# The shared expert of two sparse mixtures: four unrolled chunks become one chunk and a loop of three, on three engines, with one buffer of activations

## The chip, the cores and the metric

The kernel runs on one core of one Trainium2 chip (trn2). The metric is the device time of one execution in microseconds. TensorE is called PE here (its weight loads PEld), VectorE DVE, ScalarE ACT, GpSimd POOL and SyncE SP. A trailing q (PEldq, SPq) means the engine's sequencer: waits, register operations, branches and DMA issues.

## What is computed

Four layers of attention and feed-forward on x of 8 x 256 x 256 floats, that is 2048 tokens (16 tiles of 128 tokens) by 256 channels. The change lies in the feed-forward parts of the layers 2 and 3, which are mixtures of experts. Each adds a shared expert, which every token passes, and experts to which tokens are routed:

```python
# layer 2: 2 shared experts of 128 seen as one of 256, 16 routed ones, 2 a token
sh_mid = gelu(einsum('th,ehd->ted', xt, Wsh_up)); shared_out = einsum('ted,edh->th', sh_mid, Wsh_down)
...
routed_out = einsum('ted,edh->th', rt_mid * gate[:, :, None], Wrt_down)
return shared_out + routed_out
# layer 3: shared expert of 352, gated; 32 routed ones of 176, 6 a token
g = ragged_dot(xs, w_gate, group_sizes); u = ragged_dot(xs, w_up, group_sizes)
d = ragged_dot(silu(g) * u, w_down, group_sizes)
...
shared = silu(x @ sw_gate) * (x @ sw_up) @ sw_down
return expert_out + shared
```

## The kernel before

Both mixtures are built by one function, sparse_stage (a configuration for each layer). A stage runs in this order.

1. The normed tokens are transposed into norm_t. PE makes the logits, DVE ranks them and works out, for each token and each of its experts, a slot in a table of rows in DRAM (slot), and which expert each tile of 128 slots belongs to (expert_at).
2. POOL scatters the rows of the tokens into that table with indirect DMAs (L2190), 96 of them in layer 3 (16 tiles by 6 experts), 32 in layer 2. They are counted by the semaphores dispatched.
3. At the same time the shared expert runs on PE, ACT and DVE. The 2048 tokens are cut into 4 chunks of 512. The shared expert's hidden width is cut into SB blocks of 128: SB = 2 in layer 2 (256) and 3 in layer 3 (352). For a chunk c and a block k, shared_up (L1917) multiplies on PE into a PSUM bank: one bank (s_up_bank) in layer 2, two banks (s_gate_bank, then s_up_bank) in layer 3. Banks are double, one or the other by the number of the block. In layer 2 ACT applies Gelu and writes s_hidden (L2000); in layer 3 ACT applies Silu to the gate's bank (L1997) and DVE multiplies with the other bank into s_hidden (L2140). Then shared_down (L1927) multiplies the whole hidden width of the chunk back to 256 channels, in two halves (two banks y_bank, 2 tiles each), and DVE adds each half to x (L2148).
4. When all is there, PE walks through the tiles of routed rows: 47 in layer 2, 127 in layer 3 (transpose_rows L1939, up L1950, transpose_hidden L1958, down L1967). SP loads the rows of the tiles, 12 tiles ahead (L1870). In layer 3 room is short: SP loads the last part of the experts' weights (L1861, 3.4 MB) only after all four chunks of shared_down (wait on s_y_done for 2 * CHUNKS), since the activations of the shared expert lie in its place, and the rows are loaded behind it in SP's queue. In layer 2 SP waits for all blocks of shared_up before it loads rows.

The order of the shared expert's work is written out by shared_steps: up blocks of chunk c, with the down part of chunk c - 1 placed behind the first up block of chunk c. On PE, in layer 3, that is (first number the chunk, second the block): up 0,0; up 0,1; up 0,2; up 1,0; down 0; up 1,1; up 1,2; up 2,0; down 1; up 2,1; up 2,2; up 3,0; down 2; up 3,1; up 3,2; down 3. PE may begin up m (m = c * SB + k) when the block m - 2 has been taken out of its bank (semaphore s_hidden_ready). s_hidden is double, one for even and one for odd chunks. ACT and DVE may write a chunk's hidden block when the down part of the chunk before the last is done (s_y_done).

Signals between engines are semaphores, added to by the last instruction of a piece: s_gate_done and s_up_done by PE for each half of an up block, s_acted_ready by ACT, s_hidden_ready by DVE (by ACT in layer 2), s_y_done by PE for each half of a down part, shared_added by DVE.

A matrix product of two f32 operands is two passes, so the profile shows 2 MATMUL for each nc.tensor.matmul: an up block of layer 3 is x8, of layer 2 x4, a down part x24 and x16.

## Time and profile before

| what | us |
|---|---|
| three runs | 3160.33, 3177.08, 3180.0 |
| median | 3177.08 |
| the profiled execution, whole time | 3163.23 |
| its span in the trace | 3161.1 |

The profile is of one execution; its whole time is 2.1 us longer than the span and lies in the lower part of the range of the three runs. Times in rows are microseconds from the span's start. Layer 2's shared expert runs from about 1615 to 1671, layer 3's from about 2634 to 2796.

### The profile page before, as it was taken

To read this page: it belongs to the slowest core of one execution; us is meant where nothing else is said; L and a number is where in the kernel's file an instruction comes from. 1 tells how busy PE (TensorE), PEld (TensorE's weight loads), DVE (VectorE), ACT (ScalarE), POOL (GpSimd) and SP (SyncE) were. 2 spreads that over 40 slices of the span, in tenths; PEclk is the share of its full clock that TensorE was granted. 3 is DMA by queue.
4 is the path that set the end of the run, shared out by engine and by line. 5 is a ranking of instruction groups with operands and counts; after the bars stand their busy time and mean duration, and the time that the engine had idled before them with its cause. 6 is when DMAs were issued, how large, how long until landed. Compare 5 with 4: busy or idle time off the path is not lost. (4 is left out here: it accounts for less than half of the span.)

```text
span 3161.1 us, 64442 instructions
## 1 busy us (share of the span) xinstructions
PE 2631.6 (83%) x19747; PEld 2199.4 (70%) x19747; DVE 1942.0 (61%) x5952; ACT 1547.1 (49%) x4650; POOL 899.6 (28%) x800
## 2 busy tenths in 40 slices
PE   6975984899976599999949599999999984389995
PEld 5653553666654599999926499999999982157774
DVE  5666324788752788788733577777777773035554
ACT  6874222999971555555543354454444541013331
POOL 2111884201101322222244200100101015626664
PEclk9996755999986799999969799999999997589998
DMA  6012556800010101111034333332333236347776
GB/s 186 2 65 81 93 93 173 307 2 2 2 42 0 66 34 51 40 46 35 21 119 147 129 94 104 103 99 84 103 103 103 83 98 249 139 116 124 124 123 165
DMA packets 190350, 296.04 MB, mean 94 GB/s; under 512 B 29952, under 2 KB 160312, under 8 KB 186144
## 3 DMA queue, kind: packets, MB, share of 16 engines
q1 hardware_dynamic: 151136, 230.39, 22.5%
q0 software_dynamic: 38976, 62.68, 10.7%
q8 instruction: 125, 2.05, 0.3%
q14 instruction: 113, 0.93, 0.1%
HBM read 112.64 MB, written 96.44 MB: 66 GB/s over the span
## 5 line engine op out<-in xcount | busy, mean ns | idle before, releaser
L584 PE MATMUL bank<-norm_t_high,w 128*128 128x256 f32 (+1 forms) x2176 | 445.6, 287 | 8.3 <-DVE w L766 8.3
L732 ACT ACTIVATE probs<-bank,neg_max 128x256 f32<-128x256 f32 (+1 forms) x512 | 224.5, 443 | 395.4 <-DVE inv L841 386.5
L584 PEld LDWEIGHTS bank<-norm_t_high,w 128*128 128x128 f32 x2176 | 362.3, 193 | 8.9 <-issue 8.9
L1150 ACT ACTIVATE probs<-neg_scores,bound 128x256 f32<-128x256 f32 (+1 forms) x768 | 366.9, 486 | 2.0 <-DVE bound L1221 1.5
L584 PE MATMUL bank<-norm_t_low,w 128*128 128x256 f32 (+1 forms) x1088 | 309.4, 284 | 0.0
L1221 DVE CUSTOM_DVE_ANT_0 neg_scores<-bank,table 128x256 f32<-128x256 f32 (+1 forms) x768 | 261.7, 397 | 56.9 <-PE bank L1062 56.9
L870 POOL TENSOR_TENSOR summed<-turned 128x512 f32<-128x512 f32 x64 | 82.5, 1290 | 710.1 <-DVE turned L792 710.1
L2197 POOL DMA_INDIRECT sums<-shared,norm_t x127 | 198.1, 1560 | 177.1 <-ACT shared L2017 174.0
L642 PE MATMUL bank<-k,q 128*128 128x256 f32 (+1 forms) x1536 | 245.0, 296 | 0.0
L847 DVE SCALAR_TENSOR_TENSOR x_sb<-bank,inv,x_sb 128x256 f32 (+1 forms) x512 | 224.3, 480 | 24.4 <-DVE inv L841 13.9
L740 ACT ACTIVATE probs_t<-bank 128x384 fp32r<-128x384 f32 (+1 forms) x256 | 139.5, 545 | 200.8 <-PE bank L652 200.3
L584 PE MATMUL bank<-w,out_t 128*128 128x256 f32 x1536 | 227.0, 283 | 9.3 <-DVE out_t L833 9.2
L669 PE MATMUL bank<-probs_t,v 128*128 128x256 f32 (+1 forms) x1536 | 218.7, 278 | 4.2 <-issue 2.1
L1950 PE MATMUL bank<-weights,x_t 128*128 x696 | 206.6, 420 | 5.2 <-DVE x_t L2153 1.1
L584 PEld LDWEIGHTS bank<-norm_t_low,w 128*128 128x128 f32 x1088 | 210.6, 194 | 0.0
L584 PEld LDWEIGHTS bank<-w,out_t 128*128 128x128 f32 x1536 | 201.7, 190 | 12.6 <-DVE out_t L833 10.8
L642 PEld LDWEIGHTS bank<-k,q 128*128 128x128 f32 x1536 | 197.0, 191 | 10.2 <-issue 0.2
L669 PEld LDWEIGHTS bank<-probs_t,v 128*128 128x128 f32 x1536 | 199.2, 190 | 6.8 <-issue 3.2
L1074 PE MATMUL bank<-ident_sb,probs 128*128 128x128 f32 x1408 | 192.6, 278 | 12.7 <-ACT probs_t L1157 12.6
L1074 PEld LDWEIGHTS bank<-ident_sb,probs 128*128 128x128 f32 x1408 | 155.0, 141 | 58.3 <-issue 29.9
L1258 POOL TENSOR_SCALAR k_placed<-k_t,place 128x512 f32<-128x512 f32 x48 | 74.3, 1564 | 379.5 <-ACT k_t L1124 379.5
L1229 DVE COPY probs_t<-bank 128x512 f32<-128x512 f32 (+1 forms) x192 | 123.5, 643 | 77.4 <-PE bank L1074 76.8
(394 smaller groups left out, 5993.5 us busy)
## 6 DMA issues: line engine op xcount, KB each, us to landing
z<-norm_t_high SPq DMA_DIRECT2D x96, 256.0 KB, 2.5
z<-norm_t_low SPq DMA_DIRECT2D x96, 256.0 KB, 2.5
rows<-blank SPq DMA_DIRECT2D x1, 21336.0 KB, 65.1
norm_t<-rows SPq DMA_DIRECT2D x127, 168.0 KB
q_turned<-halves SPq DMA_DIRECT2D x256, 64.0 KB
k_turned<-halves SPq DMA_DIRECT2D x256, 64.0 KB
staged<-in_attention SPq DMA_DIRECT2D x12, 1280.0 KB, 6.4
weights<-in_experts SPq DMA_DIRECT2D x1, 13376.0 KB
```

The lines of the kernel that those rows point to most:

```text
L584: ins = nc.tensor.matmul(out, stationary(a), moving(c), start=(kt == 0 and m == 0), stop=(kt == n - 1 and m == 2))
L642: ins = nc.tensor.matmul(s[:, score_columns(causal, t)], qq[a][:, j, t * P:(t + 1) * P], kk[c][:, kj, 0:width], start=False, stop=(n == 2 ...
L669: ins = nc.tensor.matmul(o_bank[:, to], vv[a][:, kt, jv * P:(jv + 1) * P], pp[c][:, of], start=(kt == 0 and n == 0), stop=(kt == QT - 1 an ...
L732: ins = nc.scalar.activation(probs[j % 2][:, t, 0:width], s_bank[j % 2][:, score_columns(causal, t)], ACT.Exp, bias=neg_max[j % 2][:, t:t ...
L740: nc.scalar.activation(probs_t[j % 2][0][:], t_bank[:, 0:NB], ACT.Copy).then_inc(t_high, 1)
L847: ins = nc.vector.scalar_tensor_tensor(tile, y_bank[j % 2][:, t * C:(t + 1) * C], inv[j % 2][:, t:t + 1], tile, ALU.mult, ALU.add)
L1074: ins = nc.tensor.transpose(t_bank[g % 2][:, at:at + P], probs[q % 2][g][:, t, kt * P:(kt + 1) * P], core.ident[:])
L1150: ins = nc.scalar.activation(probs[q % 2][g][:, t, 0:width], neg_scores[g][:, t, 0:width], ACT.Exp, bias=bound[q % 2][:, g, t:t + 1], scal ...
L1221: ins = nc.vector.tensor_tensor_reduce(out=neg_scores[g][:, t, 0:width], in0=s_bank[g][:, t * S:t * S + width], in1=table[:, at:at + width ...
L1229: nc.vector.tensor_copy(probs_t[q % 2][g][:], t_bank[1][:, 0:NB]).then_inc(t_by_dve, 1)
L1950: ins = nc.tensor.matmul(up_bank[e % 2][:, 0:COLUMNS], x_t[e % 2][:, kt, :], weights[:, kt * COLUMNS:][:, bass.ds(expert[e], COLUMNS)], st ...
L2197: nc.gpsimd.indirect_dma_start(scratch.results[e % len(scratch.results)], bass.IndirectOffsetOnAxis(ids, 0), product[e % OUT_RING], None, ...
```

## The change

shared_steps now emits chunk 0 as straight code and the chunks 1 to 3 as the body of a loop (Fori) on each of PE, ACT and DVE, so semaphore values and addresses that depend on the chunk are worked out in registers. The down part of a chunk stands directly behind its own last up block, and no longer behind the first up block of the next chunk. s_hidden is one buffer: DVE (ACT in layer 2) writes the hidden blocks of chunk c when both halves of the down part of chunk c - 1 are done (s_y_done at 2 * c). Banks and s_acted go by k, not by m: in layer 3, with three blocks, two blocks in a row (the last of a chunk and the first of the next) now use the same bank, and what PE waits for before an up block is blocks_before(c, k) = c * SB + max(k - 1, 0) blocks taken out. PE's order in layer 3 is now up 0,0; 0,1; 0,2; down 0; up 1,0; 1,1; 1,2; down 1; and so on. The number of products, activations, additions, semaphore signals and DMAs is the same, as are POOL's and SP's programs.

```diff
...
-    def shared_steps(up, down):
-
-
-        for c in range(CHUNKS):
+    def shared_steps(eng, up, down):
+        def chunk(c):
             for k in range(SB):
                 up(c, k)
-                if k == 0 and c:
-                    down(c - 1)
-        down(CHUNKS - 1)
+            down(c)
+        chunk(0)
+        with eng.Fori(1, CHUNKS) as c:
+            chunk(c)
+    def blocks_before(c, k):
+        return c * SB + max(k - 1, 0)
...
         shared_room = Arena(weights, early_weights) if cfg.crowded else Arena(early.tensor, 0)
-        s_hidden = [shared_room.take(P, [SB, CHUNK]) for _ in range(2)]
+        s_hidden = shared_room.take(P, [SB, CHUNK])
         s_acted = [shared_room.take(P, [CHUNK]) for _ in range(2)] if cfg.gated else None
...
                 def shared_up(c, k):
-                    m = c * SB + k
-                    if m == 0:
+                    if isinstance(c, int) and k == 0:
                         pe.wait_ge(shared_loaded, 16)
-                    need(pe, s_hidden_ready, m - 1)
-                    tokens = slice(c * CHUNK, (c + 1) * CHUNK)
+                    need(pe, s_hidden_ready, blocks_before(c, k))
                     for u, (to, done) in enumerate(((s_gate_bank, s_gate_done), (s_up_bank, s_up_done))[2 - shared_ups:]):
...
                             at = ((k * shared_ups + u) * KT + kt) * P
-                            ins = nc.tensor.matmul(to[m % 2][:], shared[:, at:at + P], norm_kt[:, kt, tokens], start=(kt == 0), stop=(kt == KT - 1))
+                            ins = nc.tensor.matmul(to[k % 2][:], shared[:, at:at + P], norm_kt[:, kt, bass.ds(c * CHUNK, CHUNK)], start=(kt == 0), stop=(kt == KT - 1))
                         ins.then_inc(done, 1)
...
                                 at = shared_down_at + k * C
-                                ins = nc.tensor.matmul(y_bank[j][:, (t % 2) * C:(t % 2 + 1) * C], s_hidden[c % 2][:, k, t * P:(t + 1) * P],
+                                ins = nc.tensor.matmul(y_bank[j][:, (t % 2) * C:(t % 2 + 1) * C], s_hidden[:, k, t * P:(t + 1) * P],
                                                        shared[:, at:at + C], start=(k == 0), stop=(k == SB - 1))
...
-                shared_steps(shared_up, shared_down)
+                shared_steps(pe, shared_up, shared_down)
                 pe.wait_ge(zeroed, 1)
...
                     act.wait_ge(s_gate_done if cfg.gated else s_up_done, m + 1)
-                    if m == 0:
+                    if isinstance(c, int) and k == 0:
                         act.wait_ge(expert_ready, 1)
                     if cfg.gated:
-                        need(act, s_hidden_ready, m - 1)
-                        nc.scalar.activation(s_acted[m % 2], s_gate_bank[m % 2][:], cfg.act).then_inc(s_acted_ready, 1)
+                        need(act, s_hidden_ready, blocks_before(c, k))
+                        nc.scalar.activation(s_acted[k % 2], s_gate_bank[k % 2][:], cfg.act).then_inc(s_acted_ready, 1)
                     else:
-                        need(act, s_y_done, 2 * (c - 1))
-                        nc.scalar.activation(s_hidden[c % 2][:, k, :], s_up_bank[m % 2][:], cfg.act).then_inc(s_hidden_ready, 1)
+                        need(act, s_y_done, 2 * c)
+                        nc.scalar.activation(s_hidden[:, k, :], s_up_bank[k % 2][:], cfg.act).then_inc(s_hidden_ready, 1)
...
-                shared_steps(shared_activate, lambda c: None)
+                shared_steps(act, shared_activate, lambda c: None)
                 act.wait_ge(zeroed, 1)
...
                     dve.wait_ge(s_up_done, m + 1)
-                    need(dve, s_y_done, 2 * (c - 1))
-                    nc.vector.tensor_tensor(s_hidden[c % 2][:, k, :], s_acted[m % 2], s_up_bank[m % 2][:], ALU.mult).then_inc(s_hidden_ready, 1)
+                    need(dve, s_y_done, 2 * c)
+                    nc.vector.tensor_tensor(s_hidden[:, k, :], s_acted[k % 2], s_up_bank[k % 2][:], ALU.mult).then_inc(s_hidden_ready, 1)
                 def add_shared(c):
-                    if c == 0:
+                    if isinstance(c, int):
                         dve.wait_ge(row_normed, COPIES * TILES)
...
                         dve.wait_ge(s_y_done, 2 * c + j + 1)
-                        tiles = x[:, c * TC + 2 * j:c * TC + 2 * j + 2, :]
+                        tiles = x[:, bass.ds(c * TC + 2 * j, 2), :]
                         nc.vector.tensor_tensor(tiles, y_bank[j][:].rearrange("p (t c) -> p t c", t=2), tiles, ALU.add).then_inc(shared_added, 1)
...
-                shared_steps(shared_gated, add_shared)
+                shared_steps(dve, shared_gated, add_shared)
                 steps_of(copy_rows, gated if cfg.gated else None, copy_hidden, None)
...
```

## Rows read from the trace of the kernel before

**Rows 1.** The profile's page: the span, and each engine's busy time

```profile
span 3161.1 us, 64442 instructions
...
PE 2631.6 (83%) x19747; PEld 2199.4 (70%) x19747; DVE 1942.0 (61%) x5952; ACT 1547.1 (49%) x4650; POOL 899.6 (28%) x800
```

**Rows 2.** Groups by line, 2634 to 2796: count, busy us, mean ns, idle before

```profile
L2190 POOL DMA_INDIRECT rows<-weights,slot x96 | 92.2, 961 | 59.8 <-DVE slot L2117 30.9 <-issue 28.9
```

**Rows 3.** Timeline of PE, layer 3: start us, us, operation, count [idle before]

```profile
2650.57 5.34 PE L1927 MATMUL bank<-shared,weights 128*128 128x256 f32 x24
2655.75 7.03 PE L1917 MATMUL bank<-norm_t,shared 128*128 128x512 f32 x16
...
2731.49 7.05 PE L1927 MATMUL bank<-shared,weights 128*128 128x256 f32 x24 [16.14 <-issue]
2738.38 1.02 PE L1917 MATMUL bank<-norm_t,shared 128*128 128x512 f32 x2
...
2765.65 3.60 PE L1917 MATMUL bank<-norm_t,shared 128*128 128x512 f32 x4 [0.39 <-issue]
2771.13 5.40 PE L1917 MATMUL bank<-norm_t,shared 128*128 128x512 f32 x8 [1.88 <-DVE weights L2140]
2776.36 5.34 PE L1927 MATMUL bank<-shared,weights 128*128 128x256 f32 x24
2781.54 7.03 PE L1917 MATMUL bank<-norm_t,shared 128*128 128x512 f32 x16
2789.41 5.45 PE L1927 MATMUL bank<-shared,weights 128*128 128x256 f32 x24 [0.84 <-DVE weights L2140]
```

**Rows 4.** Timeline of DVE, layer 3

```profile
2658.60 0.69 DVE L2148 TENSOR_TENSOR x_sb<-bank,x_sb 128x512 f32<-128x512 f32 x1 [7.08 <-remote]
2685.86 0.69 DVE L2148 TENSOR_TENSOR x_sb<-bank,x_sb 128x512 f32<-128x512 f32 x1 [26.57 <-remote]
2708.33 0.69 DVE L2140 TENSOR_TENSOR weights<-weights,bank 128x512 f32<-128x512 f32 x1 [21.78 <-remote]
...
2753.12 0.69 DVE L2140 TENSOR_TENSOR weights<-weights,bank 128x512 f32<-128x512 f32 x1 [21.69 <-remote]
2769.19 1.29 DVE L2148 TENSOR_TENSOR x_sb<-bank,x_sb 128x512 f32<-128x512 f32 x2 [15.38 <-remote]
```

**Rows 5.** Timeline of ACT, layer 3

```profile
2697.06 0.60 ACT L1997 ACTIVATE weights<-bank 128x512 f32<-128x512 f32 x1 [47.42 <-issue]
```

**Rows 6.** Timeline of POOL, the last scatter of layer 3

```profile
2754.85 0.96 POOL L2190 DMA_INDIRECT rows<-weights,slot  x1 [0.30 <-issue]
```

**Rows 7.** Chain in order of time: start us, us, what

```profile
2795.73 11.74 DMA norm_t<-rows
2808.87 2.71 PE bank L1950 x4
```

**Rows 8.** Timeline of PE, layer 2

```profile
1632.35 3.60 PE L1917 MATMUL bank<-norm_t,shared 128*128 128x512 f32 x8
1657.60 6.36 PE L1927 MATMUL bank<-shared,routing 128*128 128x256 f32 x16 [21.65 <-ACT routing L2000]
1663.80 1.88 PE L1917 MATMUL bank<-norm_t,shared 128*128 128x512 f32 x4
1666.37 3.72 PE L1927 MATMUL bank<-shared,routing 128*128 128x256 f32 x16 [0.69 <-ACT routing L2000]
1669.92 0.60 PE L1939 MATMUL bank<-ident_sb,norm_t 128*128 128x128 f32 x4
```

**Rows 9.** Timeline of ACT, layer 2

```profile
1656.95 0.60 ACT L2000 ACTIVATE routing<-bank 128x512 f32<-128x512 f32 x1 [27.26 <-remote]
1659.08 0.60 ACT L2000 ACTIVATE routing<-bank 128x512 f32<-128x512 f32 x1 [1.53 <-remote]
```

**Rows 10.** Line 415, an outer loop of attention: duration ns min/median/max

```profile
L415 PEldq FUSED_REGOPS  x8: 59/64/83, 1201.5 to 2398.2; - x8
...
L415 PEldq COMPARE_BRANCH  x8: 67/209/3552, 1326.4 to 2496.8; - x8
```

## The prediction, made before the result was known

> **What bounds the kernel now.** I read the page first: PE is busy 83% of the span, DVE 61%, POOL 28% [rows 1]. That average says nothing about the shared expert, so I then looked at the chain of waits in order of time and at the engines' timelines for the two stretches that the edit touches, about 1615 to 1671 (layer 2) and 2634 to 2796 (layer 3).
>
> Layer 3 is the surprising one. PE has all 24 matmuls of down 0 started by about 2656 and up 1,1 and 1,2 by 2663 [rows 3]. Yet DVE adds the two halves of down 0 only at 2658.60 and 2685.86, after waits of 7.08 and 26.57 us that the trace gives to a releaser it cannot name ("remote") [rows 4]. ACT waits 47.42 us and takes the next block of PE's work at 2697.06, which PE had started 40 us before [rows 5, 3]. DVE follows at 2708.33 [rows 4]. ACT and DVE take turns from there: one signal from PE is used every 11.2 us or so (2697.06 to 2708.33; for DVE 2708.33 to 2753.12 is 44.8 us for four signals). DVE's own time for an operation stays at 0.69 us, and PE reacts to DVE at once (2708.33 + 0.69, and PE's next block follows). So work is not slow; what is late is news of PE's finished work. PE itself issues at a crawl late in the stretch: of the 16 matmuls of up 2,1 and 2,2, two start at 2738.38, four at 2765.65, and the ten between take 26.2 us (2739.4 to 2765.65). At 2769.19 the stall is over: two adds stand back to back [rows 3, 4].
>
> Over the same stretch POOL issues its 96 scatters without a pause, 961 ns each and 0.3 us between them [rows 2]. The last one starts at 2754.85 [rows 6]; 95 steps of 1.265 us back, the first started at 2634.7. The stall begins some 20 us after the first scatter and ends 13.4 us after the last has issued (2769.19 - 2755.81). Layer 2 has the same picture in small: PE stands for 21.65 us before 1657.60, ACT waits 27.26 us [rows 8, 9]. I do not know the mechanism. What counts here is that the stall's end is set by POOL's scatters, whose number, order and start the edit leaves alone.
>
> So the question is how much of the shared expert is left when the stall ends. In layer 3 now: up 3,0 (2771.13), down 2 (2776.36), up 3,1 and 3,2 (2781.54), down 3 (2789.41) [rows 3]. Then SP's loads, in which the last 11.74 us of the chain are the rows, and the tiles of routed rows from about 2808 [rows 7]. Everything from there to the end is one serial run, so each microsecond that the last down part is late is a microsecond of the span.
>
> **The change part by part.** *The order on PE.* The block of the next chunk that stood ahead of each down part is gone from there. It gave PE work while the last hidden block of a chunk was being made.
>
> Layer 3. In the stall one signal passes every 11.2 us whatever the order, and the same eight signals a chunk are sent. Before, PE had up to up 2,2 done when it ended. After, in the same number of passed signals (16 are two whole chunks), down 1 is done, and up 2,0 and 2,1 may follow, but up 2,2 needs block 2,0 taken out, and DVE may write that block only when both halves of down 1 have been reported. So at 2769.2 PE holds one block less. What follows the stall:
> - up 2,2 in the place of up 3,0: 2771.13 to 2776.36, 5.23 us, at a half granted clock at first, the same;
> - a gap ahead of down 2 that did not exist. The gap ahead of down 3 is the price: two up blocks from 2781.54 take 7.03 us as modelled, down 3 starts at 2789.41 where back-to-back work (5.34 modelled and 5.18 from start to start, so 0.16 less) would have put it at 2788.41. So 1.00 us;
> - down 2: 5.18 us, the same;
> - three up blocks instead of two: (2788.41 - 2781.54) / 2 = 3.43 us more;
> - the gap and down 3, the same.
> That is 1.00 + 3.43 = 4.4 us.
>
> Layer 2. PE now waits at 1657.60 for the activation of block 2,1 of ACT; this is the first one after the stall. In the new order that released signal is of up 2,0, and down 2 needs the next, which ACT begins at 1659.08 and ends 0.60 later, 1659.7: 2.1 us later [rows 8, 9]. Down 2 keeps its 6.20 us (1657.60 to 1663.80). Then two up blocks follow instead of one: half of 3.43, 1.7 us more. The gap ahead of down 3 is in both. Together 3.8 us, and the first tile of routed rows (1669.92 now) moves by as much. SP's wait for all up blocks is met later too, but PE has the gap and down 3 (4.6 us) behind it, so the rows stay hidden.
>
> *Chunks 0 and 1*, before the stall, lose the same kind of gap. It is absorbed: the stall's end does not move by it.
>
> *The loops.* Each engine gets a move, an add and a branch an iteration and register operations for semaphore values and addresses. An outer loop of attention shows the price on PE: a register operation 64 ns, a branch 209 ns at the median and 3552 ns once in eight [rows 10]. Behind the stall there is one back edge and some 15 register operations on PE in each layer. Those ahead of queued matmuls are covered by them (PE's sequencer runs ahead of its 0.43 us matmuls); those just behind a wait are not. From below 0, from above 0.21 + 15 x 0.064 = 1.2 us a layer; I take 0.25 a layer, nearer to the covered end, since matmuls are queued at nearly all of them. DVE's and ACT's register operations fall in their idle time: 0, or under 0.3 a layer without that cover.
>
> *One buffer of s_hidden.* DVE waits for the down part of the chunk before. By PE's new order that part is issued before the next up block, so the wait costs DVE nothing outside the stall; within it, it is what limits PE to up 2,1, counted above. *Bank by k* (two blocks in a row in one bank): PE's wait for the whole chunk is already met by the down part. 0. *Shorter program*: nothing on the path.
>
> Sum: 4.4 + 3.8 + 0.5 = 8.7 us. Profiled execution: 3163.2 + 8.7 = 3171.9. The median of the three runs shown is 13.9 above the profiled one, which gives 3185.8. The runs lie at both ends (3160 and 3178 to 3180) and the profiled one at the lower, so I take the middle: 3179.
>
> **The branch, trace and page.** The row shows one taken branch of 3552 ns against 209 [rows 10]. The Trainium skill, "Runtime: NRT & Kernel Launch", section "Instruction fetch mechanics", says that a taken branch whose target lies outside the two pages held forces a fetch before execution goes on, and advises unrolling. By that page every back edge of these loops could miss; one row in eight does, so the trace agrees for a minority only.
>
> **The rivals.**
> *Every back edge misses* (5%). The body is short, some 120 instructions by its 48 + 48 of matmul and weight load, so the target has just been run; for it speaks only the one slow branch. Of two taken ones a layer the first lies in the stall; the second costs 3.55 - 0.21 = 3.3 on the path. Twice: 3179 + 7 = 3186.
> *The crawl decides* (13%): the slower side. PE ran the 24 matmuls of down 1 and two more in 7 us from 2731.49, then crawled through ten in 26.2 us and ran four at full speed [rows 3]. If block 1,2 is reported only at 2753.12, 40 matmuls (down 1, up 2,0, up 2,1) still stand before PE, and if the crawl ends with PE's own backlog instead of with POOL's, the same ten crawl: 2753.8 + 7 + 26.2 + 4 x 0.43 = 2788.7, 20 us past 2769: 3179 + 20 = 3199. Should the signals also fall one pair behind (22.4 us), 3221, which is over 1%. It decides from the point at which fewer than 14 signals have passed by 2753. Against it: the last four matmuls ran at full speed from 2765.65, when POOL had been silent for 10 us.
> *The stall shrinks or goes* (9%): the faster side. If PE's far run ahead of what is reported makes the stall, the tighter order may weaken it. Then POOL's end bounds: 2755.8 + 12.6 us of loads (down 3 ends at 2794.86, the rows are in at 2807.47) gives 2768.4 for 2807.5, 39 us [rows 3, 6, 7]. Of the 21.65 us that PE stands in layer 2 the scatters would still hold a part; I take half, 11 us. 3179 - 50 = 3129; half of it 3154. Against it: PE is idle in most of the stall and nothing improves.
> *No difference* (8%): the 8.7 us are hidden by a stall that ends earlier with one block less to report: about 3170.
>
> **Chances and range.** The sum as worked out: 65%. One per cent (32 us) is about what a measurement of this kernel can tell from no change; the three runs differ by 20. Faster by over 1%: most of the case that the stall goes, 7%. Slower by over 1%: the crawl with a pair of signals behind, and some of the rest, 9%. Within 1%: 84%. The likeliest case spans 3168 to 3190 (the two ends of the runs, with 8.7). Taking in the missed back edges, the plain crawl and a little of the shrunken stall, 3158 to 3201 should hold 8 in 10.
>
> **What would show it.** Right: POOL's last scatter of layer 3 near 2755 plus 4, the pair of adds L2148 that ends the stall 13 us later, then one up block, down, three up blocks, down, with gaps near 1 us ahead of both down parts; layer 2's first routed tile 3 to 4 us later. Wrong: a stall that ends at another distance from POOL's last scatter, adds spaced by other than 11.2 us, or PE's branch rows above 3 us.

## The result, and the profile after

The changed kernel takes 3186.51 us (median of 14 runs, 3177.38 to 3196.01), the kernel before beside it 3171.51 us (14 runs, 3160.33 to 3182.61). The ratio is 1.0045, with a 95% interval of 1.0032 to 1.0059: 10 to 19 us slower, 15.0 us by the medians. The profiled execution of after took 3187.42 us, its span is 3185.3. Two later measurements of the same kernel gave ratios of 1.0030 (1.0016 to 1.0045) and 1.0044 (1.0027 to 1.0061).

The page of after. The busy times are those of [rows 1], but for 14.5 us more of PE's and 15.3 us more of its weight loads; the mean granted clock was 0.886 against 0.894:

```profile
span 3185.3 us, 64570 instructions
...
PE 2646.1 (83%) x19747; PEld 2214.7 (70%) x19747; DVE 1942.5 (61%) x5952; ACT 1549.4 (49%) x4650; POOL 899.5 (28%) x800
```

The timeline of PE in layer 3, after (start us, us, operation, count, idle before). It answers to [rows 3]; up is now line 1921, down 1931, the first routed tile's transposes 1943:

```profile
2667.52 5.45 PE L1931 MATMUL bank<-shared,weights 128*128 128x256 f32 x24 [0.85 <-DVE weights L2144]
2672.81 7.03 PE L1921 MATMUL bank<-norm_t,shared 128*128 x16
2711.09 6.36 PE L1921 MATMUL bank<-norm_t,shared 128*128 x8 [31.26 <-issue]
2755.88 7.89 PE L1931 MATMUL bank<-shared,weights 128*128 128x256 f32 x24 [38.42 <-issue]
2763.61 5.31 PE L1921 MATMUL bank<-norm_t,shared 128*128 x12
...
2790.20 6.07 PE L1921 MATMUL bank<-norm_t,shared 128*128 x8 [10.41 <-DVE weights L2144]
2797.19 5.44 PE L1931 MATMUL bank<-shared,weights 128*128 128x256 f32 x24 [0.92 <-DVE weights L2144]
2802.47 10.46 PE L1921 MATMUL bank<-norm_t,shared 128*128 x24
2813.86 5.44 PE L1931 MATMUL bank<-shared,weights 128*128 128x256 f32 x24 [0.93 <-DVE weights L2144]
2832.01 1.08 PE L1943 MATMUL bank<-ident_sb,norm_t 128*128 128x128 f32 x4 [12.71 <-DMA norm_t<-rows]
```

The timeline of DVE there (answers to [rows 4]; 2152 adds a half of a down part, 2144 makes a hidden block), and POOL's last scatter (answers to [rows 6]):

```profile
2671.76 0.69 DVE L2152 TENSOR_TENSOR x_sb<-bank,x_sb 128x512 f32<-128x512 f32 x1 [4.29 <-PE bank L1931]
2687.79 0.69 DVE L2152 TENSOR_TENSOR x_sb<-bank,x_sb 128x512 f32<-128x512 f32 x1 [15.34 <-remote]
2710.35 0.69 DVE L2144 TENSOR_TENSOR weights<-weights,bank 128x512 f32<-128x512 f32 x1 [21.87 <-remote]
...
2755.05 0.69 DVE L2144 TENSOR_TENSOR weights<-weights,bank 128x512 f32<-128x512 f32 x1 [21.71 <-remote]
2785.21 0.69 DVE L2152 TENSOR_TENSOR x_sb<-bank,x_sb 128x512 f32 x1 [29.47 <-remote]
2788.80 0.69 DVE L2152 TENSOR_TENSOR x_sb<-bank,x_sb 128x512 f32 x1 [2.90 <-remote]
```

```profile
2774.32 0.96 POOL L2194 DMA_INDIRECT rows<-weights,slot  x1 [0.30 <-issue]
```

The stall is there as before. It ends at 2788.80, 13.5 us behind the end of POOL's last scatter (2775.28); before it was 13.4. (2788.80 is the second add of down 1, 3.59 us behind the first; before, the two stood back to back from 2769.19.) Behind it stand one up block, down 2, three up blocks (10.46 in place of 7.03) and down 3, with gaps of 0.92 and 0.93 ahead of the two down parts. From the end of the stall down 2 starts 8.39 us later (before 7.17), down 3 16.67 us after that (before 13.05), and the first routed tile 18.15 us after that (before 18.20): 4.79 us more in sum.

Layer 2, PE and ACT, answers to [rows 8, 9]:

```profile
1649.51 3.60 PE L1921 MATMUL bank<-norm_t,shared 128*128 x8
1676.60 6.50 PE L1931 MATMUL bank<-shared,routing 128*128 128x256 f32 x16 [23.50 <-ACT routing L2004]
1682.93 3.60 PE L1921 MATMUL bank<-norm_t,shared 128*128 x8
1687.30 3.72 PE L1931 MATMUL bank<-shared,routing 128*128 128x256 f32 x16 [0.77 <-ACT routing L2004]
1690.86 0.60 PE L1943 MATMUL bank<-ident_sb,norm_t 128*128 128x128 f32 x4
```

```profile
1675.37 1.08 ACT L2004 ACTIVATE routing<-bank 128x512 f32<-128x512 f32 x2 [29.56 <-remote]
```

DVE there, the two halves of down 1:

```profile
1655.17 0.69 DVE L2152 TENSOR_TENSOR x_sb<-bank,x_sb 128x512 f32 x1 [13.50 <-remote]
1671.96 0.69 DVE L2152 TENSOR_TENSOR x_sb<-bank,x_sb 128x512 f32 x1 [16.09 <-remote]
```

Down 2 waits for two activations that ACT makes back to back. POOL's scatters of layer 2 end at 1654.37 before and 1670.69 after. Down 2 starts 3.23 us behind that end before and 5.91 after; from there to the first routed tile it is 12.32 and 14.26. That is 2.7 + 1.9 = 4.6 us.

The loops themselves, by the source line of the loop, PE's part (duration ns min/median/max):

```profile
L1763 PEldq FUSED_REGOPS  x6: 41/44/46, 1637.4 to 2799.0; - x6
...
L1763 PEldq COMPARE_BRANCH  x6: 76/211/223, 1646.2 to 2815.4; - x6
```

The profiles differ by 24.2 us. 16.3 of them lie ahead of layer 2's first up block (1614.96 and 1631.26), where the code is the same. The two stretches from a layer's first scatter to its first routed tile hold 9.6. Between and behind them the changed kernel is 1.7 us shorter, again in code that is the same.

### The profile page after: what moved, and what is told of

Its sections match the earlier page's. It is cut to its first block and busy times, and to the rows that moved or that the text cites. A ratio compares the mean times of both kernels' runs of the same rounds, so it can differ in the third digit from the quotient of the medians.

```text
span 3185.3 us, 64570 instructions
## 1 busy us (share of the span) xinstructions
PE 2646.1 (83%) x19747; PEld 2214.7 (70%) x19747; DVE 1942.5 (61%) x5952; ACT 1549.4 (49%) x4650; POOL 899.5 (28%) x800
```

## The experiments

The measure for all of them, beside the medians, is read off each kernel's timelines of POOL and PE: from the first scatter of a layer to the first transposes of its first routed tile. A set is a group of kernels run together, with the kernel before beside them: four kernels in the first, four in the second, then two and two. **In sets 1 and 3 the kernel before took 3174.77 and 3171.96 us; in sets 2 and 4 3117.10 and 3116.38**: the stall is there in the one pair and missing in the other. The kernel before was profiled only once, so every difference of stretches rests on that one profile.

| kernel | layer 2, us | layer 3, us | sum against before | median against before, same set |
|---|---|---|---|---|
| before | 55.86 | 172.98 | | |
| after, three profiles | 60.49, 60.72, 60.56 | 177.90, 178.09, 177.62 | +9.6, +10.0, +9.3 | +15.0, +10.7, +14.4 |
| order_unrolled | 58.55 | 178.02 | +7.7 | +8.9 |
| two_buffers_again | 60.07 | 178.13 | +9.4 | +14.4 |
| loop_old_order | 60.45 | 177.57 | +9.2 | +11.7 |
| old_order_one_buffer | 55.61 | 176.46 | +3.2 | +3.3 |
| order_two_buffers (set 2) | 44.21 | 127.38 | | 0.0 |

### Set 1: which part costs what

The changed kernel again, as a yardstick.

> The changed kernel once more, as the yardstick of this set. By its first measurement it is 10 to 19 us behind the kernel before. In the two profiles at hand 16.3 us of their difference lie ahead of the changed code (layer 2's first up projection starts at 1614.83 and 1631.13), 3.2 us in layer 2's shared expert and 4.9 us in layer 3's. If the early 16.3 us are chance between executions, the new profile has layer 2's first up projection anywhere between 1610 and 1635, and the median stays 8 to 14 us behind. If they come from the change, it lies near 1631 again.

Measured: 3185.48 us (12 runs), ratio 1.0030 (1.0016 to 1.0045). Layer 2's first up block starts at 1627.14, neither near 1631 nor near 1615.

The new order with the loop written out:

```diff
-        with eng.Fori(1, CHUNKS) as c:
+        for c in range(1, CHUNKS):
             chunk(c)
```

> The new order and the one buffer, with the three loops written out. Theory of the order (mine): the shared expert loses 3 us in layer 2 and 4 to 5 us in layer 3 by the order alone, the loops cost 0.5 us, so this kernel is 8 us behind the kernel before, ratio near 1.0026. Theory of the loops: whatever is over 8 us in the measured 14 us comes with the loops, here then 8 us against 14 us in the kernel with loops. Theory that all 14 us are the order: ratio 1.0045 here too, with no loop in it.

Measured: 3183.71 us, ratio 1.0023 (1.0011 to 1.0035), +8.9 us. The theory of the order gave +8; +15, the theory that all is the order, lies outside the interval (3 to 11 us). But the two stretches show only 1.6 to 2.2 us between this kernel and the one with loops, nearly all in layer 2. Two things make it up there. Down 2 starts 5.19 us behind POOL's last scatter and not 5.91, since one of the two activations was made earlier (1666.57 and 1672.17). And down 2 takes 5.1 us to the next block and not 6.3, at a granted clock of 0.69 in place of 0.56.

The old order in a loop:

```diff
         def chunk(c):
             for k in range(SB):
                 up(c, k)
-            down(c)
+                if k == 0 and not (isinstance(c, int) and c == 0):
+                    down(c - 1)
 
         chunk(0)
-        with eng.Fori(1, CHUNKS) as c:
+        chunk(1)
+        with eng.Fori(2, CHUNKS) as c:
             chunk(c)
+        down(CHUNKS - 1)
```

> The old order (each down projection behind the next chunk's first up block) with one buffer and the banks taken by k, chunks 2 and 3 in a loop on the three engines, chunks 0 and 1 written out. A first up block in the loop waits for all blocks of the chunk before, as in the changed kernel. Theory of the order: 0 to 1.5 us behind the kernel before (loops 0.25 us in each layer, that wait up to 0.5 us in each), ratio 1.0000 to 1.0005. Theory of the loops: about 6 us behind, ratio near 1.002, and layer 2's first up projection late in the profile as in the changed kernel.

Measured: 3186.48 us, ratio 1.0034 (1.0023 to 1.0045), +11.7 us. A clear miss of my theory, which gave 0 to 1.5. The theory of the loops gave 6, also too little, and its mark (layer 2 starting late) has nothing to do with it: the start was 1622.87. The timeline of PE shows where it goes:

```profile
1642.83 1.88 PE L1924 MATMUL bank<-norm_t,shared 128*128 x4
1668.22 3.77 PE L1924 MATMUL bank<-norm_t,shared 128*128 x4 [23.52 <-ACT routing L2007]
1671.79 4.68 PE L1934 MATMUL bank<-shared,routing 128*128 128x256 f32 x16
...
2787.87 6.48 PE L1924 MATMUL bank<-norm_t,shared 128*128 x8 [12.50 <-DVE weights L2147]
2795.28 3.69 PE L1924 MATMUL bank<-norm_t,shared 128*128 x8 [0.93 <-DVE weights L2147]
2798.81 5.34 PE L1934 MATMUL bank<-shared,weights 128*128 128x256 f32 x24
```

Here it is an up block (1668.22, 2795.28) that waits for the last hidden block of the chunk before, as the down part does in the changed kernel. `blocks_before` asks for all blocks of that chunk, the kernel before asked for one less, so that an up block could run while the last hidden block was made. With that wait, the old order saves nothing: 60.45 and 177.57 against 60.49 to 60.72 and 177.62 to 178.09. I had named the wait in the expectation and sized it at half a microsecond a layer. The experiment mixes it with the loop and with the one buffer, and can't price any of them alone.

One buffer in the old order:

```diff
-        s_hidden = [shared_room.take(P, [SB, CHUNK]) for _ in range(2)]
+        s_hidden = shared_room.take(P, [SB, CHUNK])
...
-                        need(act, s_y_done, 2 * (c - 1))
+                        need(act, s_y_done, 2 * c)
```

(DVE's wait likewise.)

> The kernel before with one buffer of activations in place of two, nothing else. My account puts the buffer at nothing: activation and product of a chunk's first block would wait for the down projection ahead of them, which in the stall lies between them anyway. But the old order runs up block 0 ahead of the down projection, and its activation now waits until that projection is done: 0.6 us and what hangs on it, up to 2 us a layer. So 0 to 4 us, ratio 1.0000 to 1.0013. A rival in which the second buffer is what keeps the stalled stretch going gives 10 us and more.

Measured: 3178.10 us, ratio 1.0016 (1.0007 to 1.0025), +3.3 us, within my range of 0 to 4. The rival of 10 us falls. The place was only half right: nothing in layer 2 (-0.25), 3.5 us in layer 3. PE's timeline there, behind the stall:

```profile
2773.89 9.73 PE L1917 MATMUL bank<-norm_t,shared 128*128 128x512 f32 x16 [23.04 <-DVE weights L2140]
2783.46 5.34 PE L1927 MATMUL bank<-shared,weights 128*128 128x256 f32 x24
2788.64 7.03 PE L1917 MATMUL bank<-norm_t,shared 128*128 128x512 f32 x16
2796.51 5.45 PE L1927 MATMUL bank<-shared,weights 128*128 128x256 f32 x24 [0.84 <-DVE weights L2140]
```

The stall ends 13.5 us behind POOL's last scatter (2759.58 to 2773.11), and then two up blocks stand ahead of down 2, where [rows 3] have one. DVE may not write block 2,0 before down 1 is reported, so PE gets one block less far in the stall. That is the mechanism of the prediction, in a kernel where only the buffer is changed.

### Set 2: a set in which no signal is late

The new order written out with two buffers (`s_hidden[c % 2]`, waits on `2 * (c - 1)`). The edit also changed one line elsewhere that looks the same: in fixed_experts_stage, which runs once at about 310 to 360 us, DVE's product at L1594 waits for `2 * (c - 1)` too, though that stage has a single s_hidden. Its four products lie 35.0 and 34.5 us apart, first to last, in the two runs of this kernel, against 34.8 before and 34.6 after. So the times say nothing of it, and it lies ahead of both stretches; but it is a wait that protects a buffer, and the kernel is not to be copied with it.

> The new order written out, with two buffers of activations (block c % 2) as in the kernel before; banks by k. From layer 2's and layer 3's first up projection to the first routed tile the profiles so far give 54.8 and 173.3 us (before), 54.5 and 176.7 (one buffer in the old order), 57.4 and 178.3 (new order and one buffer, written out). My account by the prediction: in the new order the buffer costs nothing, since a down projection stands between the chunks anyway, so this kernel equals the written-out one: 57.4 and 178.3. The rival: the 3.5 us that the one buffer costs in layer 3 come off again, which leaves 57.4 and 175 and a median some 4 us ahead of the written-out kernel with one buffer.

Measured: 3117.07 us against 3117.10 for the kernel before, ratio 1.0000 (0.9989 to 1.0011). The kernel before is 57.7 us faster than in set 1, for the stall is not there. PE's timeline of layer 3:

```profile
2638.70 13.03 PE L1921 MATMUL bank<-norm_t,shared 128*128 128x512 f32 x24
2652.59 5.45 PE L1931 MATMUL bank<-shared,weights 128*128 128x256 f32 x24 [0.85 <-DVE weights L2144]
2657.87 10.46 PE L1921 MATMUL bank<-norm_t,shared 128*128 128x512 f32 x24
...
2702.35 5.45 PE L1931 MATMUL bank<-shared,weights 128*128 128x256 f32 x24 [0.84 <-DVE weights L2144]
2766.39 1.08 PE L1943 MATMUL bank<-ident_sb,norm_t 128*128 128x128 f32 x4 [58.59 <-DMA norm_t<-rows]
```

No wait in the shared expert is over 0.85 us, its last down part starts at 2702.35, and the routed tiles start 6.2 us behind POOL's last scatter (2760.21). From first scatter to first routed tile that is 11.6 us less in layer 2 and 45.6 in layer 3 than in the kernel before [rows 8, 3]: 57.2 us, and that is the 57.7 by which the medians of the kernel before differ, but for 0.5. So the stall accounts for the whole difference between the sets.

The first two up blocks ahead of the wait for the routing (the small products of the routing go to other banks for it):

```diff
+                for k in range(2):
+                    shared_up(0, k)
+
                 pe.wait_ge(chosen_ready, 1)
```

> The kernel before, with the first two up blocks of the shared expert issued ahead of TensorE's wait for the chosen experts, in the idle time of the routing (8.35 us in layer 2, 14.77 us in layer 3); the places and counts go to banks 6 and 7 for that. GpSimd's scatters start where they did. If the end of the stall is set by GpSimd's last scatter and what counts is the work left by then, the work moved comes off at its undisturbed price, two blocks of 3.5 us: 5 to 7 us in layer 2 and 5 to 7 us in layer 3, in sum 10 to 14 us faster, ratio 0.9955 to 0.997. If the stalled stretch instead ends with a given amount of work done whatever was there before it, nothing or under 2 us is gained in layer 3 and the first scatter's place alone decides.

Measured: 3117.70 us, ratio 0.9998 (0.9988 to 1.0008). All of it is covered here, since POOL's scatters end 60 us after the shared expert. It doesn't tell the two theories apart.

The scatters held back:

```diff
+                pool.wait_ge(s_y_done, 2 * CHUNKS)
                 for n, (t, k) in enumerate(sends):
```

> The kernel before, with GpSimd's scatters of both layers held until the shared expert's last down projection is done. If the scatters are what delays TensorE's signals, no wait in the shared expert is longer than 3 us, layer 3's takes 70 to 90 us from first up to last addition (four times 3 blocks of 3.5 us and a down of 5.3 us are 63 us, at a clock of 0.5 to 1), layer 2's 35 to 45 us, and then 96 and 32 scatters of 1.265 us follow, 121 and 40 us: the kernel is 40 to 90 us slower in all. If the stall has another cause (the loads of the weights, the clock), waits of 10 to 20 us stay in the shared expert.

Measured: 3209.89 us in one run, 92.8 over the kernel before. The shared expert takes 66 us in layer 3 (2658.76 to the end of the last down part) and 30 in layer 2, with no wait over 0.84 us. But it has none in this set with the scatters beside it either, so nothing follows for the cause. What it does give is a price: laying scatters and shared expert side by side saves 92.8 us where nothing is late, about the shared expert's whole 66 + 30.

Narrow matmuls:

```diff
-                        for kt in range(KT):
+                        for q in range(4):
+                            part = slice(q * P, (q + 1) * P)
+                            for kt in range(KT):
```

(each matmul then writes `to[m % 2][:, part]` from the columns `part`.)

> The kernel before, with each up projection's matmul of 512 columns made four of 128, so that half a block is 16 matmuls and 16 weight loads of TensorE in place of 4 and 4, for the same columns and the same one signal. In the stall a half now takes 11.2 us. If a signal has that price, or if it goes by columns, it stays 11.2 us (layer 3's down halves, 16.1 us for 3072 columns against 11.2 for 2048, speak for columns). If it goes by TensorE's instructions it takes 25 to 45 us, and much less of the shared expert is done when the scatters end: layer 3 then loses 20 us and more. Outside the stall the loads cost some, 1 us a block.

Measured: 3118.47 us in one run, no block late, 3.57 us a block in place of 3.43 (10.72 against 10.30 for three). Inconclusive on the stall, for the same reason.

### Sets 3 and 4

> The new order written out with two buffers, once more: the set before ran on a chip on which no signal of TensorE was late and the kernel before took 3117 us; there this kernel stood at 1.000 of it. If this set's chip has the late signals (the kernel before near 3175 us, layer 3 at 173 us from first up to first routed tile): 178.3 us in layer 3 and some 8 us behind if the one buffer costs nothing in the new order, 175 us and some 4 us behind if its 3.5 us come off. If it has none: 1.000 again, layer 2 at 43.3 us and layer 3 at 127.7 us.

Measured: 3186.39 us, ratio 1.0039 (1.0022 to 1.0056); the signals are late in this set. Layer 3 takes 178.13 us against 178.02 with one buffer (order_unrolled, set 1). (The expectations count from the layer's first up block and not from the first scatter; by that measure it is 178.43, where 178.3 stood for "the buffer costs nothing" and 175 for the rival.) So in the new order the second buffer buys nothing in layer 3, and the rival falls. This kernel has no loop and is not ahead of the one with loops, so most of the 2 us that order_unrolled had seemed to gain in layer 2 (58.55) are not the loop's: without a loop it is 58.55 once and 60.07 once. Down 2 shows why: it starts 5.19 and 5.31 us behind POOL's last scatter, but then runs at a granted clock of 0.69 in the one profile and 0.53 in the other.

> The changed kernel again, beside the one above. On a chip with the late signals: 10 to 14 us behind the kernel before, 59.5 us in layer 2 and 178.3 us in layer 3. On a chip without them the shared expert lies wholly beside GpSimd's scatters (its last down projection starts at 2702.35, the scatters end at 2760.21), so order, buffer and loops are all covered: ratio 1.000, within 2 us. A rival: the loops cost something outside the shared expert (the program's length), then 3 us and more are left there too.

Measured: 3186.34 us, ratio 1.0044 (1.0027 to 1.0061), 60.56 and 177.62 us. As expected for late signals, but for layer 2, where 59.5 was expected. The changed kernel itself never ran in a set without them, so that its ratio is 1.000 there is inferred from the kernel with two buffers and no loop.

A version meant to beat both: early_ups, and layer 3's last weights in three loads.

```diff
+                if cfg.crowded:
+                    sp.wait_ge(expert_ready, 1)
+                    at = slice(shared_room.at, rows_at)
+                    sp.dma_start(weights[:, at], weights_in[:, at]).then_inc(weights_loaded, 16)
                 for i in range(PORTIONS):
-                    if cfg.crowded and i == PORTIONS - 1:
-                        sp.wait_ge(s_y_done, 2 * CHUNKS)
...
+                sp.wait_ge(s_up_done, (CHUNKS - 1) * SB)
+                for e in range(early_rows):
...
+                        sp.wait_ge(s_y_done, 2 * done)
```

> The kernel before, with two things. First, the first two up blocks ahead of the wait for the chosen experts, as in the kernel tried above. Second, layer 3's last load of weights (27136 bytes a partition, issued when the last down projection is done; the first routed tile's transposes start 12.76 us after the last addition) in three parts: what lies behind the shared expert's activations as soon as the experts are chosen, the first buffer's part when down projection 2 is done, the rest (40% of it) at the end; and the first four token tiles' rows are loaded ahead of that. On a chip with late signals my theory (the stall ends 13.5 us behind GpSimd's last scatter, and what counts is the work left then) gives 4 to 7 us in layer 2, 4 to 7 us in layer 3's shared expert, and the gap of 12.76 us becomes 6 to 8: in sum 13 to 20 us faster than the kernel before, ratio 0.994 to 0.996. If the stall takes back what is started early, only the gap's 5 us remain, 0.9985. On a chip without late signals the shared expert is done 50 us before the scatters, and all of it is covered: 1.000.

Measured: 3122.48 us, ratio 1.0016 (1.0004 to 1.0028), 6.1 us slower, in a set without late signals. I expected 1.000. SP's timeline shows my mistake:

```profile
2660.13 91.35 SPq L1866 DMA_DIRECT2D weights<-in_experts  x4
2751.53 1.85 SPq L1870 DMA_DIRECT2D norm_t<-rows  x4
2753.43 1.15 SPq L1874 DMA_DIRECT2D weights<-in_experts  x2
```

The last two parts of the weights now stand behind SP's waits for the scatters. The shared expert had been done since 2690, but they go out at 2753.43, and the larger lands 8.5 us later; the first routed tile comes 13.5 us behind POOL's last scatter in place of 6.2. The kernel before waits for the last down part ahead of its last wait for scatters, and so loads in their shadow. Each of the two orders is right where the other event is the late one. Whether this version wins with late signals wasn't tried.

> The kernel before with each up matmul of 512 columns made four of 128, once more, since the first time ran on a chip without late signals (there layer 3 took 128.2 us and no block was late). On a chip with late signals: half a block's signal stays 11.2 us apart if the price goes by signals or by columns, and layer 3 stays at 173 to 180 us; it is 25 to 45 us if the price goes by TensorE's instructions, less is done when the scatters end, and layer 3 takes 190 us and more.

Measured: 3111.15 us in one run, again in a set without late signals (127.9 us by the measure of the expectation). Whether the price of a late signal goes by instructions or by columns stays open as far as this experiment goes.

## Why the prediction came out as it did

**Layer 3, 4.4 us.** It held. The gap ahead of down 2 was put at 1.00 and came to 1.22 (8.39 - 7.17). The third up block was put at 3.43 and came to 3.62. Sum 4.84, and 4.6 to 5.1 over three profiles from the first scatter. The assumption behind it, that PE stands after up 2,1 and not after up 2,2 when the stall ends, is in the rows: 12 matmuls at 2763.61 and four that crawl are up 2,0 and 2,1.

**Layer 2, 3.8 us.** It held in kind, 4.6 to 4.9 in size. The added up block was put at 1.7 and came to 1.9. The wait for the second activation was put at 2.1 and came to 2.7. The prediction read 2.1 off the distance between the two signals that ACT uses when the stall ends, 1656.95 and 1659.08. Counted from the end of POOL's last scatter (1654.37) these are 2.58 and 4.71 us. In the changed kernel ACT begins 4.68 us behind that end, which fits the later of the two. What the prediction missed is that the signal ahead of it is used no earlier either, so ACT then has two activations to make and not one, some 0.5 us more. In the two unrolled kernels the first of the two is made ahead of time, and down 2 is 2.0 and 2.1 us later than before, as predicted.

**That POOL sets the stall's end.** In layer 3 the distance from the end of POOL's last scatter to the end of the stall, measured at ACT's first activation behind it, is 13.56 us before, 13.53 with one buffer, 13.52 in loop_old_order, 13.20 written out, 13.54 with two buffers, and 13.45, 13.49 and 13.58 in the three of after. Over eight profiles of six kernels that is as good as a constant. Layer 2 has another distance, and it goes with the kernel: the ACT row that releases PE there starts 2.58 us behind the last scatter in both kernels of the old order without a loop, and 4.5 to 4.8 in the six other profiles. So there what is queued on PE has a say too. That POOL's scatters cause the stall is argued from this and not shown: the kernel that holds them back ran only where nothing was late.

**"One signal every 11.2 us."** Wrong as worded. In layer 3 the two halves of down 0 are used 16.0 us apart after (2671.76 and 2687.79), and up halves 11.2 (11.04 to 11.36). A half of layer 3's down is 12 matmuls of 256 columns, 3072, an up half 4 of 512, 2048; in layer 2 a down half is 8 of 256, again 2048, and its adds were 11.25 us apart before (1636.61 and 1647.86). So these spacings follow the work behind the signal, 5.2 to 5.5 ns a column, and not the signal. But not all do. In layer 2 the halves of down 1, 2048 columns, are 16.8, 16.8 and 17.5 us apart in the three profiles of after. In layer 3 DVE uses no signal between 2755.05 and 2785.21, 30.2 us for 3072 columns, and then one 3.59 us later; before, the halves of down 0 are 27.3 us apart (2658.60 and 2685.86). By the prediction's own list that is a sign of being wrong ("adds spaced by other than 11.2 us"): the rate of the signals was not known, only where PE stands when the stall ends. The sum survived since it hangs on that alone, and since POOL's end and not the rate sets the end in layer 3.

**One buffer, 0.** Right in the new order: 178.13 us with two against 178.02 with one in layer 3. The prediction said that PE's order makes the wait free. The counterpart shows it: in the old order, where it isn't, the buffer costs 3.5 us of layer 3. The order and the buffer each take PE the same one block in the stall, so they don't add.

**Bank by k, 0.** Right only as long as the down part stands ahead. In loop_old_order, where it doesn't, the wait for the whole chunk together with the one buffer and the loop costs 9.2 us, against 3.2 for the one buffer alone. The other 6.0 are the bank's wait and the loop; that they are the wait is read from the timeline and not shown by a run of its own. The new order costs nearly everything by itself (9.4 us in two_buffers_again, which has two buffers and no loop), the one buffer a third.

**Loops, 0.5 us.** On PE the branches that go back took 209 to 223 ns, those that leave the loop 76 and 83, none near the 3.55 us of the rival in which each misses. (Two of the eight branches in [rows 10] leave their loop as well, at 67 ns; so one of six that go back is slow there, where the prediction says one in eight.) The Trainium skill, "Runtime: NRT & Kernel Launch", section "Instruction fetch mechanics", advises unrolling because of that fetch. These short loops show no such fetch, so it can be left undone here: behind the stall the gaps ahead of the down parts grow by 0.08 us (0.92 against 0.84), and the kernel with loops and the unrolled one with two buffers stand at 3186.34 and 3186.39 us in one set. Only the loop's first pass in layer 2 shows more, a gap of 1.52 to 2.06 us ahead of down 1 where the unrolled kernels have 0.69, and the stall covers it.

**From the sum to the time.** This is the step that missed, by 7.5 us. The sum was 8.7 and the stretches show 9.3 to 10.0. But I put the forecast midway between 3163.2 + 8.7 and the median + 8.7, at 3179, which is 2 us above the median of before and no longer the sum. The profiled execution was at the low end of all runs of before. It also has a granted clock of 1.00 over its first 200 us, where the three of after have 0.92 to 0.94. This varies without any change. One and the same kernel, with two buffers in the new order, shows 0.92 once and 0.99 once (busy us and count by engine, then the clock), and reaches layer 2's first up block at 1630.24 and 1622.94:

```profile
0.00:200.00 200.00, 158.82 (x1579) 124.45 (x1580) 117.41 (x570) 148.43 (x552) 42.44 (x42) 0.92 0.26 75
```

```profile
0.00:200.00 200.00, 159.38 (x1655) 123.78 (x1656) 123.82 (x599) 154.17 (x580) 42.41 (x42) 0.99 0.26 75
```

The 16.3 us ahead of the changed code are of this kind: the profiles of all kernels, in which that code is the same, reach this block between 1615 and 1633, the three with a clock of 0.99 or 1.00 at 1614.96, 1618.87 and 1622.94, those with 0.97 and 0.98 at 1622.81, 1622.87 and 1628.12, those with 0.92 to 0.94 at 1621 to 1633. The clock of that start goes with the time only loosely, and what else makes the 16.3 us isn't shown. 8.7 on the median of all the runs of before (3171.5 to 3174.8) is 3180 to 3184, and 3186.5 was measured. What the median shows beyond the stretches is 5.4, 0.7 and 5.1 us for the changed kernel, and 5.0 for the one without a loop in the same set as the last, so it isn't the loops. In the first measurement the stretches' 9.6 lie just below the interval (10 to 19 us), in the others inside. In all seven comparisons of the table it is above zero (0.1 to 5.4). If the one profile of before were long in its stretches, that would follow; no second profile of it with the stall is there to settle it.

**The rivals.** The crawl went on as the prediction wanted, 12 matmuls fast and four slow, and didn't decide. The stall neither shrank nor went with the change of order. It goes altogether in some sets, with the kernel unchanged, and there the forecast of "no difference" is the true one for order and buffer (ratio 1.0000, 0.9989 to 1.0011). The prediction never asked whether the stall belongs to the kernel at all. That was the largest thing it missed, 57 us beside the 9 that it worked out. Here it was luck that it didn't matter: the profile and the measurement both had the stall. Without it both kernels would stand near 3117 us, outside the range of 3158 to 3201.

## What to carry to other kernels

When a stretch has waits that the trace can't assign, look first at whether they come back in another set of runs; a cost worked out inside such a stretch holds only where the stretch exists. Price an order of work by what is queued on the engine when the stall ends, count blocks, and add the buffer's and the bank's waits once where they take away the same block. Put the sum on the median of many runs, not on the profiled execution, and compare granted clocks ahead of the changed code before calling a difference the change's.

## What the runs showed of the hardware

The stall is a property of the set of runs, not of the kernel. All profiles of sets 1 and 3 and of the first measurement have it, none of sets 2 and 4, and the times of the other runs say the same: none of the former is under 3157 us, and none of the latter over 3128 but for the kernel that holds the scatters back. Sets 3 and 4 bear the same chip number, so if that names one chip it isn't fixed to it either. POOL issues alike in both, 96 scatters of 961 ns in 121.2 us, and DMA moves the same bytes. What differs besides the time is the trace's own record of signals. The DMA view of the kernel before from 2635 to 2755 (queue: packets, MB, share; issues, with the median us to landing at the end where there is one), then that of the new order with two buffers in set 2 from 2639 to 2759:

```profile
q0 software_dynamic: 4512, 16.18, 35.6%
...
rows<-weights,slot POOLq DMA_INDIRECT x96
```

```profile
q0 software_dynamic: 4512, 16.18, 35.4%
...
rows<-weights,slot POOLq DMA_INDIRECT x95, 2.5
```

In the first no landing can be given, since most of the records of the scatters' signals are missing: 216 are left in that window, against 1488 in the other. Over the whole trace all eight profiles with the stall hold 29,437 to 29,674 records of signals, and all six without it 33,634 to 33,668. So late signals of PE and lost records of signals come together, 8 of 8 and 0 of 6. The Trainium skill, "NOTIFIC — the notification-queue block", section 7.1 ("Overflow: three behaviours, one of which stalls the engine"), says that the block which writes such records can, as it is set, drop them when a ring is full, and that it holds the producer back when its own pipeline is full. The trace has both symptoms, lost records and held-back work, and can't show the block. Whether the recording makes the stall, or both have another cause, stays open: each run here has its span and clock from such records, so none can tell. So does why a set has it.

A second thing is open, and the prediction and this text speak as if it were settled. "Signals come late" is one reading; the other is that PE's matmuls themselves end late. The trace gives their starts, and their ends are modelled. For the second speaks the crawl. These are its first and last matmul before, and then after:

```profile
2740.45 0.59 PE L1917 MATMUL bank<-norm_t,shared 128*128 128x512 f32 x1 [1.05 <-issue]
...
2764.25 1.01 PE L1917 MATMUL bank<-norm_t,shared 128*128 128x512 f32 x1 [1.09 <-issue]
```

```profile
2770.38 0.59 PE L1921 MATMUL bank<-norm_t,shared 128*128 x1 [1.46 <-issue]
...
2778.78 1.01 PE L1921 MATMUL bank<-norm_t,shared 128*128 x1 [1.09 <-issue]
```

The ten of 512 columns before start 2.64 us apart on average, which is 5.2 ns a column, the four after 2.8 us apart, 5.5 ns. That is the spacing of the signals, 5.2 to 5.5 ns a column, and undisturbed it is 0.43 us a matmul. The granted clock doesn't explain it: it was 0.60 from 2740 to 2765 before and 0.72 from 2770 to 2780 after, and even its lower level, 0.50, would be a factor of two and not of six.
